# Context attention without GpSimd: the maxima subtracted by VectorE, the row sums shared by VectorE and TensorE

## The reference

```
x = x + xattn(layernorm(x), ctx)   # one head: q = x wq, keys and values = 4096 rows of ctx
                                   #   and 256 new rows (x wk, x wv); softmax(q k / sqrt(512)) v, times wo
x = x + attn(layernorm(x))         # 16 heads, low-rank queries, keys and values, rotary part, causal
x = x + moe(layernorm(x))          # 32 routed experts, 8 per token, and a shared expert
```

## Time and profile before

| | |
|---|---|
| median of three runs | 537.16 us (534.91 to 544.28) |
| profiled execution | 535.09 us, span from first to last instruction 533.2 us |
| mean granted TensorE clock | 0.99 |
| busy: TensorE, VectorE, ScalarE, GpSimd | 509.7, 420.0, 301.7, 73.3 us |

### The profile page before, as it was taken

How to read it: one execution, slowest core, us unless ns; L and a number is a source line. 1 busy time by engine, 2 the same in 40 slices (tenths; PEclk the granted TensorE clock), 3 DMA queues, 4 the chain that set the end, 5 groups by cost and what they waited for, 6 DMA issues and landing times.

```text
span 533.2 us, 10271 instructions
## 1 busy us (share of the span) xinstructions
PE 509.7 (96%) x3780; PEld 473.0 (89%) x3780; DVE 420.0 (79%) x614; ACT 301.7 (57%) x438; POOL 73.3 (14%) x62
## 2 busy tenths in 40 slices
PE   9999997579998999998999999999999999999997
PEld 7999987579877988977989999999999999999997
DVE  6776679999779887877797777877768778687675
ACT  5755656536447766764736464565654655646632
POOL 1000009992154131101000000000000000000000
PEclk9999998989999999999999999999999999999999
DMA  8775622326621242260636546456465564564621
GB/s 291 280 233 179 210 89 80 118 81 203 198 74 36 82 143 74 92 235 1 236 119 237 186 169 232 162 197 203 163 225 184 170 230 155 205 199 165 226 70 39
DMA packets 19461, 86.26 MB, mean 162 GB/s; under 512 B 2160, under 2 KB 2416, under 8 KB 19312
## 3 DMA queue, kind: packets, MB, share of 16 engines
q1 hardware_dynamic: 19440, 85.99, 47.9%
HBM read 85.46 MB, written 0.52 MB: 161 GB/s over the span
## 4 chain that ended last, share of the span: by engine, by line
PE 71%; DVE 16%; DMA 4%; issue 4%; ACT 4%; SPq 0%; POOL 0%; DVEq 0%; ACTq 0%
PE bank L1001 31%; PE bank L443 10%; PE bank L447 9%; PE bank L446 9%; DVE w_lo L296 7%; PE bank L451 3%; PE bank L455 3%; PE bank L454 3%; DMA raw<-w_mla_dram 3%; ACT w_hi L291 1%; DVE operands L1402 1%; DMA raw<-ctx_t_dram 1%; DVE score_rows L1538 1%; ACT score_rows L1122 1%; DVE xt_lo L344 1%
## 5 line engine op out<-in xcount | busy, mean ns | idle before, releaser
L291 ACT CAST w_hi<-raw 128x768 fp32r<-128x768 f32 (+3 forms) x158 | 159.5, 1040 | 113.5 <-PE bank L1001 82.4
L296 DVE TENSOR_TENSOR w_lo<-raw,w_hi 128x1280 fp32r<-128x1280 f32 (+3 forms) x156 | 204.5, 1353 | 14.0 <-ACT w_hi L291 12.8
L1001 PE MATMUL bank<-xt_hi,w_lo 128*128 128x256 f32 x512 | 105.3, 277 | 0.0
L1001 PE MATMUL bank<-xt_hi,w_hi 128*128 128x256 f32 x512 | 105.3, 277 | 0.0
L1001 PE MATMUL bank<-xt_lo,w_hi 128*128 128x256 f32 x512 | 105.1, 277 | 0.0
L1001 PEld LDWEIGHTS bank<-xt_hi,w_hi 128*128 128x128 f32 x512 | 81.8, 188 | 2.7
L1001 PEld LDWEIGHTS bank<-xt_lo,w_hi 128*128 128x128 f32 x512 | 79.7, 188 | 0.0
L1001 PEld LDWEIGHTS bank<-xt_hi,w_lo 128*128 128x128 f32 x512 | 79.7, 188 | 0.0
L443 PE MATMUL bank<-w_hi,operands 128*128 128x512 f32 (+1 forms) x194 | 75.1, 387 | 1.6 <-DVE operands L344 1.0
L447 PE MATMUL bank<-w_hi,operands 128*128 128x512 f32 (+1 forms) x194 | 74.1, 382 | 0.0
L446 PE MATMUL bank<-w_lo,operands 128*128 128x512 f32 (+1 forms) x194 | 73.8, 380 | 0.0
(11 more groups left out here) (200 smaller groups left out, 888.6 us busy)
## 6 DMA issues: line engine op xcount, KB each, us to landing
raw<-w_exp_dram SPq DMA_DIRECT2D x34, 896.0 KB, 4.8
raw<-w_exp_dram SPq DMA_DIRECT2D x34, 640.0 KB, 5.6
raw<-ctx_t_dram SPq DMA_DIRECT2D x16, 512.0 KB, 4.8
raw<-ctx_n_dram SPq DMA_DIRECT2D x16, 512.0 KB, 3.7
raw<-w_mla_dram SPq DMA_DIRECT2D x8, 512.0 KB, 3.6
raw<-w_mla_dram SPq DMA_DIRECT2D x8, 448.0 KB, 4.0
raw<-wq_dram SPq DMA_DIRECT2D x4, 256.0 KB, 5.2
raw<-wk_dram SPq DMA_DIRECT2D x2, 512.0 KB, 7.2
```

What stands on the lines that cost most here:

```text
L291: act.copy(w_hi[:, t.slot, at:at + n], raw[:, t.slot, at:at + n]).then_inc(hi_split[k], 1)
L296: eng.tensor_tensor(w_lo[:, t.slot, at:at + n], raw[:, t.slot, at:at + n], w_hi[:, t.slot, at:at + n].bitcast(F32), ALU.subtract) \
L1001: return pe.matmul(bank[b + u][:, m * T:m * T + T], a[:, t.slot, at + m * P:at + m * P + P], x[:, c, :], start=c == 0 and a is w_hi and x ...
```

## The change

GpSimd does nothing in the context attention any more. VectorE subtracts the maxima of groups 2 to 7 too, always one group ahead of the group whose low parts it makes. The row sums are made from two sides. Of each group's four blocks of keys, VectorE adds the first two into `parts`. The other two are multiplied by TensorE with a matrix of 1/128, high part and low part, in two matmuls of 512 columns, which sum into bank 0 (`add_up` is now TensorE's); the new keys go that way too. Every partition of bank 0 then holds 1/128 of the sum over the keys, so that the later sum over 128 partitions counts it once. `total_rows` adds bank 0 to `parts`, then the two halves. ScalarE's copy of the maxima goes, and its order changes: the exponential of group g+1 and the cast of that group's first half now stand at the end of group g.

```
+            def add_up(hi, lo, first=False, last=False):
+                pe.matmul(bank[0][:, :], shares[:, :], flat(hi), start=first, stop=False)
+                ins = pe.matmul(bank[0][:, :], shares[:, :], flat(lo), start=False, stop=last)
+                if last:
+                    ins.then_inc(bank_full[0], 1)
...  times_first, ahead of the products of its fourth block
+                    if k == 3:
+                        pe.wait_ge(ones_rounded, 1)
+                        add_up(pt_hi[:, 0, 2:4, :], pt_lo[:, 0, 2:4, :], first=True)
...  times_new, at its end
+                add_up(new_pt_hi[:, :, :], new_pt_lo[:, :, :])
...  times_context, ahead of its products (and so in times_last, with last=True)
                 pe.wait_ge(ev_lo, j * 2 + (V_P1 + s - 1))
+                add_up(pt_hi[:, s % 2, 2:4, :], pt_lo[:, s % 2, 2:4, :])
...  ScalarE
             act.wait_ge(lowered, 5)
-            act.copy(top_all, bank[1][:, T:2 * T]).then_inc(top_shared, 1)
             exps(score_rows[:, 1024:2048])
             probs_hi(5, flat(pt_hi[:, 1, :, :]), score_rows[:, 1024:2048])
             split_hi(act, Tile(0, T_CN + 1), 1, X_SIZES)
+            act.wait_ge(lowered, 6)
+            exps(score_rows[:, 2048:3072])
+            split_hi(act, Tile(0, T_CN + 2), 0, X_SIZES)
             for g in range(2, NG):
                 t = Tile(0, T_CN + g)
-                v = score_rows[:, g * 1024:g * 1024 + 1024]
-                act.wait_ge(lowered_late, g - 1)
-                exps(v)
-                split_hi(act, t, 0, X_SIZES)
                 act.wait_ge(used[1], t.free(1))
-                probs_hi(g + 4, flat(pt_hi[:, g % 2, :, :]), v)
+                probs_hi(g + 4, flat(pt_hi[:, g % 2, :, :]), score_rows[:, g * 1024:g * 1024 + 1024])
                 split_hi(act, t, 1, X_SIZES)
+                if g + 1 < NG:
+                    act.wait_ge(lowered, g + 5)
+                    exps(score_rows[:, g * 1024 + 1024:g * 1024 + 2048])
+                    split_hi(act, Tile(0, T_CN + g + 1), 0, X_SIZES)
...  VectorE (its loop over pairs of groups before had split_lo, probs_lo, split_lo)
+            lower(by_keys(2048, 4), 4)
+            dve.tensor_tensor(parts[:, :, :], by_keys(0, 2), by_keys(1024, 2), ALU.add).then_inc(summed, 1)
+            split_lo(dve, Tile(0, T_CN + 2), 0, X_SIZES)
+            for g in range(2, NG):
+                if g + 1 < NG:
+                    lower(by_keys((g + 1) * 1024, 4), 4)
+                probs_lo(V_P1 + g - 1, pt_hi[:, g % 2, :, :], pt_lo[:, g % 2, :, :], by_keys(g * 1024, 4))
+                split_lo(dve, Tile(0, T_CN + g), 1, X_SIZES)
+                dve.wait_ge(summed, g - 1)
+                dve.tensor_tensor(parts[:, :, :], parts[:, :, :], by_keys(g * 1024, 2), ALU.add).then_inc(summed, 1)
+                if g + 1 < NG:
+                    split_lo(dve, Tile(0, T_CN + g + 1), 0, X_SIZES)
...  total_rows
-                dve.wait_ge(summed, NG)
-                dve.tensor_tensor(total_parts[:, 0:2, :], total_parts[:, 0:2, :], total_parts[:, 2:4, :], ALU.add) \
-                   .then_inc(totals, 1)
+                dve.wait_ge(summed, NG - 1)
+                dve.wait_ge(bank_full[0], F0["shares"])
+                dve.tensor_tensor(parts[:, :, :], parts[:, :, :], bank[0][:, :].rearrange("p (k t) -> p k t", k=2),
+                                  ALU.add).then_inc(totals, 1)
...  GpSimd
+            pool.memset(shares.bitcast(F32)[:, :], 1.0 / P).then_inc(ones_rounded, 1)
-            def lower(g):
...
-            def add_up(g):
...
```

More of the change, by code:

```diff
@@ L72 @@
 C_END = C_TIE + 2 * GROUPS * GROUPS
-F01 = dict(ln1=1, s_even=2, ln2=8, rope=9, y=10, ln3=11, h_t=12, moe=12)
-F0 = dict(s_new=6, sums=7)
-F1 = dict(tops=6, top_all=7)
+F01 = dict(ln1=1, s_even=2, ln2=9, rope=10, y=11, ln3=12, h_t=13, moe=13)
+F0 = dict(s_new=6, shares=7, sums=8)
+F1 = dict(tops=7, top_all=8)
 F23 = dict(q=1, s_odd=2, o=6, qkv=7, rope=8, scores=9, pt=10, ln3=25, moe=25)
@@ L140, in perceiver_layer @@
         rope_raw = sb("rope_raw", [P, 4, 512])[:, :, :]
-        tops = sb("tops", [P, 4, T])
+        tops = sb("tops", [P, 3, T])
+        parts = sb("parts", [P, 2, T])
         rw_hi = sb("rw_hi", [P, NC, E], F32R)
@@ L153, in perceiver_layer @@
         q_root = sb("q_root", [P, 2])
+        shares = sb("shares", [P, P], F32R)
         apart = sb("apart", [P, 56])
@@ L198, in perceiver_layer @@
         new_keys = by_keys(CTX * 2, 2)
-        top_pair, top, top_all = tops[:, 0:2, :], tops[:, 2, :], tops[:, 3, :]
-        total_parts = xn[:, :, :].rearrange("p h (k t) -> p (h k) t", t=T)
+        top_pair, top = tops[:, 0:2, :], tops[:, 2, :]
         def row(at, n):
@@ L242, in perceiver_layer @@
         zeroed = sem("zeroed")
+        ones_rounded = sem("ones_rounded")
         rw_split = sem("rw_split")
@@ L252, in perceiver_layer @@
         top_row_ready = sem("top_row_ready")
-        top_shared = sem("top_shared")
         lowered = sem("lowered")
-        lowered_late = sem("lowered_late")
         p_ready = sem("p_ready")
@@ L565, in transpose_tops @@
                 for h in range(2):
-                    ins = pe.transpose(bank[1][:, half(h)], top[:, half(h)], ident)
-                ins.then_inc(bank_full[1], 1)
+                    pe.transpose(bank[1][:, half(h)], top[:, half(h)], ident).then_inc(bank_full[1], 1)
             def share_tops():
@@ L641, in transpose_totals @@
                 for h in range(2):
-                    ins = pe.transpose(bank[0][:, half(h)], total_parts[:, 0, half(h)], ident)
+                    ins = pe.transpose(bank[0][:, half(h)], parts[:, 0, half(h)], ident)
                 ins.then_inc(bank_full[0], 1)
@@ L649, in times_last @@
                 pe.wait_ge(ev_lo, V_P1 + s - 1)
+                add_up(pt_hi[:, s % 2, 2:4, :], pt_lo[:, s % 2, 2:4, :], last=True)
                 for m in range(NC):
@@ L1433, in total_rows @@
             def total_rows():
-                dve.wait_ge(summed, NG)
-                dve.tensor_tensor(total_parts[:, 0:2, :], total_parts[:, 0:2, :], total_parts[:, 2:4, :], ALU.add) \
-                   .then_inc(totals, 1)
+                dve.wait_ge(summed, NG - 1)
+                dve.wait_ge(bank_full[0], F0["shares"])
+                dve.tensor_tensor(parts[:, :, :], parts[:, :, :], bank[0][:, :].rearrange("p (k t) -> p k t", k=2),
+                                  ALU.add).then_inc(totals, 1)
                 dve.wait_ge(totals, 1)
-                dve.tensor_tensor(total_parts[:, 0, :], total_parts[:, 0, :], total_parts[:, 1, :], ALU.add) \
-                   .then_inc(totals, 1)
+                dve.tensor_tensor(parts[:, 0, :], parts[:, 0, :], parts[:, 1, :], ALU.add).then_inc(totals, 1)
                 dve.wait_ge(bank_full[0], F0["sums"])
@@ L1817, in _ @@
                 root(h + 1, h, 1)
-            def lower(g):
-                v = by_keys(g * 1024, 4)
-                pool.tensor_tensor(v, v, top_all.unsqueeze(1).broadcast_to([P, 4, T]), ALU.subtract) \
-                    .then_inc(lowered_late, 1)
-            def add_up(g):
[L1827 to L1844, removed]
             pool.wait_ge(lo_split[0], Tile(0, T_QKV).split(0))
```

## The result

The kernel after takes 521.42 us (median of four, 521.37 to 522.39), the kernel before 536.39 us (median of four, 534.91 to 544.28): a ratio of 0.9734, 95% interval 0.9711 to 0.9758, so 2.7% faster. The forecast was 522.4 us, its range 517 to 530. The profiled run took 521.37 us, against a sum of 521.5.

The account below looks back on a forecast made before the run. VectorE, slowed while GpSimd works, was taken to pace the context attention. With TensorE pacing at 5.90 us per group the projection starts 13.6 us earlier: 521.5 from the profiled run, 523.6 from the median, forecast 522.4 us, range 517 to 530.

Parts of the forecast that it names:

- VectorE back to 1.21 us: Context attention: with GpSimd idle, each 1024-wide VectorE instruction falls from 3.3 to 1.21 us.
- The subtraction of the maxima at 1.22 us on VectorE: Per context group, VectorE takes over a 1024-wide subtraction with the maxima in PSUM, costing 1.22 us.
- VectorE's group, 5.5 us: VectorE's work per context group: four 1024-wide instructions at 1.21 us plus a 0.68 us addition, 5.5 us.
- the pacer rival: VectorE still paces the context groups, waiting for ScalarE's casts: 527.2 us with one wait per group, 534 with two; chance 0.14.
- Eighteen products at 0.23 us, 4.1 us: TensorE's added 512-column products for the row sums start 0.23 us apart, adding 4.1 us in all.
- TensorE's group, 5.90 us: TensorE's time per context group: 5.44 us plus 0.46 us for the added pair of products, 5.90 us.
- One wait of about 1.0 us at group 2, from 89.5 to 90.5: TensorE waits once, ahead of context group 2, for the low parts of the probabilities, about 1.0 us.
- The projection at 126.1: The output projection after the context attention starts at 126.1 us instead of 139.75, 13.6 us earlier.
- The sums don't delay the end, DMA costs nothing: Final row sums take VectorE 3.5 us, before the transposes are asked for at 4.5; DMA loads add nothing.
- The rest moved as a block: Everything from the output projection on, some 393 us, keeps its queues and buffers and only shifts earlier.
- the clock: Rival: TensorE's clock falls to half after the group 2 wait; 524.0 us if once, 527 if three times; chance 0.07.
- slowness by its own load: Rival: VectorE's 3.3 us instructions come from its own full load, so groups take 15 us; 575 us, chance 0.04.

Follow-up runs that it names:

- gpsimd_reads: Kernel after plus eleven 1024-column additions on GpSimd, on a spare buffer, whose results nobody needs; 541.13 us.
- sums_moved_alone: Kernel after with the subtractions of groups 2 to 7 and the copy of the maxima back on GpSimd, row sums still on VectorE and TensorE; 538.64 us.
- gpsimd_writes: Kernel after plus 36 memsets of 1024 columns on GpSimd, on a spare buffer, so that it only writes; 522.19 us.
- subs_moved_alone: Kernel after with the row sums back on GpSimd and no products with 1/128, subtractions still on VectorE; 528.56 us.

## Why the prediction was right

The sum met the profiled time to 0.1 us, and that is luck in part: the start was 0.40 us later than laid out, the stage 0.3 us longer and the rest 0.67 us shorter, which cancel. What the prediction had right is the mechanism: VectorE's short instructions come back and TensorE sets the pace.

- **VectorE back to 1.21 us**: 1.22 in after, and shown by intervention: reads bring the long instructions back (2.91 us), writes don't (1.22).
- **The subtraction of the maxima at 1.22 us on VectorE**: 1220 ns. The forecast took the price from a time when GpSimd rests; gpsimd_reads shows that it would have held beside GpSimd's reads too.
- **VectorE's group, 5.5 us**: too long. It added durations, but instructions on VectorE start before the one ahead has ended: casts' low parts stand at 1.23 us and start 1.13 after. The first cast's low part of a group starts at 92.27, 97.40 and 102.54 us, 5.14 apart. So the slack per group was 0.8 us, not 0.4, which made the pacer rival less likely than I had it.
- **Eighteen products at 0.23 us, 4.1 us**: 0.24 apart, 4.3 us. The 131 ns of the page "TensorE: Matmul & The Clock Gate" of the Trainium skill, section "Back-to-back issue gap", weren't seen here; the estimate by it was 2.4 us.
- **TensorE's group, 5.90 us**: 5.92 to 5.94 in four windows. Group 2 took 6.22 with the same work and no wait; its 256-column products start (96.78 - 91.24) / 47 = 0.118 us apart, those of group 3 (102.69 - 97.36) / 47 = 0.113.
- **One wait of about 1.0 us at group 2, from 89.5 to 90.5**: 0.52 us, until 90.67. VectorE was 0.2 us later than laid out; TensorE came later by more, as its group 1 began at 83.86 (83.6 forecast) and ran at 0.118 too.
- **The projection at 126.1**: 126.82, with a start 0.40 us later; the stage is 52.10 against 126.1 - 74.32 = 51.8.
- **The sums don't delay the end, DMA costs nothing**: no wait in the last two windows; 158 to 212 GB/s in the groups.
- **The rest moved as a block**: 392.8 us instead of 393.5. In this run that held. It was a weaker step than I took it for: gpsimd_reads and sums_moved_alone lost 6 us there.

The rivals: VectorE did not become the pacer, the clock did not fall (1.00 in every window), and slowness by its own load is refuted, as VectorE is full in the 96.89 and 102.81 windows of after at 1.22 us.

## What to carry to other kernels

GpSimd is no free helper beside VectorE when GpSimd reads SBUF and VectorE's instructions have two inputs there: take the duration of one VectorE shape with GpSimd busy and with it idle, from the same trace, and charge GpSimd's work with the difference. Work worth 5.2 us of this stage on VectorE and TensorE cost 18.5 us of it when GpSimd did it. Where work is shared between two engines, give the one that has time left per group as much as it can take without coming late, and only the rest to the one that sets the pace.

## What was not expected of the hardware

TensorE has two paces at the same granted clock of 1.00: 256-column products start 0.113 or 0.118 us apart. It changes within a stage (groups 2 and 3 above) and can hold for a long time. The window of sums_moved_alone from 350 to 400 us shows 358 products with no gap; the same stretch of before shows 369:

```profile
350.00:400.00 50.00, 50.00 (x369) 47.05 (x368) 37.87 (x44) 29.00 (x34) 0.00 (x0) 1.00 0.56 189
```

The ten profiled runs other than sums_moved_alone and gpsimd_reads, before's among them, show 366 to 369 there, and gpsimd_reads 358. From the projection's start to the end the two runs with 358 take 399.4 and 399.1 us (spans 536.8 and 539.3 less 137.40 and 140.21), the ten others 392.6 to 393.5. Set against after's, matmul by matmul from the end, both lose 0.6 us in every 25 us of the last 250. So this pace is what sums_moved_alone lost behind its stage, and why gpsimd_reads took 19 us more than gpsimd_writes with a stage only 13.2 us longer. What selects the pace stays open. Long waits in the stage alone don't, as subs_moved_alone, with waits up to 4.3 us, shows 369 in that window too. Both cases are single runs, so it isn't shown either that their edits brought it about.
